# One fused two-layer kernel: the queries of head h+4 moved ahead of the scores of head h+2

## What is computed

```python
x += expert(layernorm(x), ...)      # int8-like quantised linear, SiLU gate, quantised linear
x += bitlinear_ffn(layernorm(x))    # 704 hidden units, ternary weights
x += cross_attention(layernorm(x), ctx, Wq, Wk, Wv, Wo)   # 16 heads of 128, 8 key/value heads
x += shared_ffn(layernorm(x)) + top2_routed_ffn(layernorm(x))  # 1024 hidden units, 128 routed
```

## Time and profile before

| | |
|---|---|
| median of three runs | 385.16 us |
| the profiled execution | 384.46 us |
| its span, from its first to its last instruction | 382.7 us |
| granted TensorE clock | 0.999 of full speed |
| TensorE (PE) busy | 373.5 us, 98% |
| TensorE weight loads (PEld) busy | 352.6 us, 92% |
| VectorE (DVE) busy | 299.0 us, 78% |
| ScalarE (ACT) busy | 233.8 us, 61% |
| GpSimd (POOL) busy | 163.1 us, 43% |

### The profile page before, as it was taken

How to read it: one execution, slowest core, us unless ns; L and a number is a source line. 1 busy time by engine, 2 the same in 40 slices (tenths; PEclk the granted TensorE clock), 3 DMA queues, 4 the chain that set the end, 5 groups by cost and what they waited for, 6 DMA issues and landing times.

```text
span 382.7 us, 8393 instructions
## 1 busy us (share of the span) xinstructions
PE 373.5 (98%) x2966; PEld 352.6 (92%) x2966; DVE 299.0 (78%) x983; ACT 233.8 (61%) x617; POOL 163.1 (43%) x260
## 2 busy tenths in 40 slices
PE   8899999999999999999999999999999999999996
PEld 7788799999899989999999999999999989999896
DVE  4798889899867889887867999787767876766644
ACT  1798787877644466767454567766554666764232
POOL 2113876947533345345353445246343243332232
PEclk9999999999999999999999999999999999999999
DMA  7999200000000300000000200000000000000000
GB/s 241 340 376 399 79 33 2 2 2 0 3 2 0 87 0 3 2 1 3 0 29 2 60 1 2 0 3 1 3 29 2 0 3 0 3 0 2 15 17 27
DMA packets 15193, 16.93 MB, mean 44 GB/s; under 512 B 1584, under 2 KB 14128, under 8 KB 15152
## 3 DMA queue, kind: packets, MB, share of 16 engines
q1 hardware_dynamic: 15152, 16.40, 12.8%
HBM read 15.34 MB, written 1.05 MB: 43 GB/s over the span
## 4 chain that ended last, share of the span: by engine, by line
PE 83%; DVE 9%; ACT 3%; POOL 2%; issue 1%; DVEq 0%; POOLq 0%
PE bank_qa L412 12%; PE bank_u L649 8%; PE bank_o L668 8%; PE bank_pt L633 7%; PE bank_s L613 7%; PE bank_s L412 5%; PE bank_o L672 4%; PE bank_u L653 4%; PE bank_s L621 4%; PE bank_s L531 3%; PE bank_pt L412 2%; PE bank_u L757 2%; PE bank_pt L531 2%; PE bank_x L421 2%; PE bank_pt L561 2%; PE bank_x L757 1%
## 5 line engine op out<-in xcount | busy, mean ns | idle before, releaser
L1339 POOL TENSOR_SCALAR prob<-prob,row_inv,valid_b 128x256 f32<-128x256 f32 x128 | 71.0, 566 | 82.7 <-DVE row_inv L1710 82.7
L1034 ACT ACTIVATE prob<-prob,row_min 128x256 f32<-128x256 f32 x128 | 64.1, 503 | 41.7 <-DVE row_min L1702 41.4
L1715 DVE TENSOR_TENSOR pt_lo<-bank_pt,pt_hi 128x512 fp32r<-128x512 f32 x64 | 43.8, 685 | 14.3 <-ACT pt_hi L987 14.3
L1702 DVE CUSTOM_DVE_ANT_0 prob<-bank_s,masked 128x256 f32<-128x256 f32 x128 | 48.5, 416 | 0.9 <-ACT masked L1016 0.6
L1350 POOL TENSOR_TENSOR act_lo<-act_raw,act_hi 128x256 fp32r<-128x256 f32 x32 | 24.2, 756 | 44.0 <-ACT act_hi L1102 43.9
L633 PE MATMUL bank_pt<-ident,prob 128*128 128x128 f32 x256 | 39.3, 275 | 0.6 <-DVE pt_lo L1715 0.6
L987 ACT ACTIVATE pt_hi<-bank_pt 128x512 fp32r<-128x512 f32 x64 | 37.6, 587 | 3.9 <-PE bank_pt L633 3.7
L613 PE MATMUL bank_s<-cxT_hi,qa_hi 128*128 128x256 f32 x128 | 37.7, 317 | 0.0
L412 PE MATMUL bank_qa<-xt_hi,a_hi 128*128 128x256 f32 x126 | 35.1, 279 | 0.0
L412 PE MATMUL bank_qa<-xt_lo,a_hi 128*128 128x256 f32 x126 | 35.1, 279 | 0.0
L412 PE MATMUL bank_qa<-xt_hi,a_lo 128*128 128x256 f32 x126 | 35.1, 279 | 0.0
(11 more groups left out here) (338 smaller groups left out, 1187.9 us busy)
## 6 DMA issues: line engine op xcount, KB each, us to landing
wq_raw<-in_wqT SPq DMA_DIRECT2D x4, 512.0 KB, 7.6
wo_raw<-in_wo SPq DMA_DIRECT2D x4, 512.0 KB, 7.7
w_raw<-in_w12T SPq DMA_DIRECT2D x2, 704.0 KB, 7.4
gate_raw<-in_gateT SPq DMA_DIRECT2D x2, 576.0 KB, 7.3
up_raw<-in_upT SPq DMA_DIRECT2D x2, 576.0 KB, 9.9
down_raw<-in_downT SPq DMA_DIRECT2D x2, 576.0 KB, 11.8
x<-in_x SPq DMA_DIRECT2D x4, 256.0 KB, 5.0
guT<-in_guT SPq DMA_DIRECT2D x4, 256.0 KB, 3.3
```

What stands on the lines that cost most here:

```text
L1034: act.activation(row, row, ACT.Exp, scale=-1.0, bias=row_min[:, h % 2, t:t + 1], accum_out=row_sum[:, h % 2, t:t + 1]).then_inc(S["s_exp"], 1)
L1339: pool.tensor_scalar(row, row, row_inv[:, h % 2, t:t + 1], valid_b[:, 0:1], ALU.mult, ALU.mult).then_inc(S["s_norm"], 1)
L1702: dve.tensor_tensor_reduce(out=prob[:, h % 2, t, :], in0=src[:, t * T:(t + 1) * T], in1=masked[:, :], scale=1.0, scalar=3.0e38, op0=ALU.ad ...
L1715: dve.tensor_tensor(pt_lo[:, :, cols], bank["pt"][:, :].rearrange("p (s t) -> p s t", s=2), f32(pt_hi[:, :, cols]), ALU.subtract).then_inc ...
```

## The change

In each turn of TensorE's attention loop the queries of head h+4 stand directly behind the transposes of head h, and the scores of head h+2 behind them. No instruction is added or removed, and no engine but TensorE has another order. The wait for `qa_l` in front of an even head's queries now stands ahead of the scores. The scores' own waits move with them.

```diff
@@ -677,10 +677,10 @@
 
                 for h in range(H):
                     turn_probs(b, h)
+                    if h + 4 < H:
+                        queries(b, h + 4)
                     if h + 2 < H:
                         scores(b, h + 2)
-                    if h + 4 < H:
-                        queries(b, h + 4)
                     if beside is not None:
                         beside(h, 0)
                     if h >= 2:
```

## The result

The changed kernel took 385.98 us, the median of 11 runs (385.66 to 386.71), beside 385.00 us for the kernel before in the same session. The ratio is 1.0026, with a 95% interval of 1.0018 to 1.0034: 1.0 us slower, where 0.7 was forecast. The profiled execution has a span of 383.9 us at a granted clock of 1.0, against 382.7 before.

The account below looks back on a forecast made before the run. TensorE, busy 98% of the span, was taken to bound the kernel. Terms 0.6 (batch 3) + 0.05 + 0.05 (batches 1 and 2) + 0 (batch 0) = 0.7 us, giving 385.16 + 0.7 = 385.9 us, range 384.9 to 387.0.

Parts of the forecast that it names:

- Batch 3, 0.6 us forecast: Turns 0 and 2: queries wait for `qa_lo` (0.59 and 0.34 us), minima 0.43 us late; 0.6 us stay to the end.
- The hole before turn 3: Batch 3: TensorE's idle time before the transposes of turn 3 takes back 0.2 us of its 0.79 us lateness.
- Batch 1, 0.05 us forecast: Turn 2's queries wait 0.16 us for `qa_lo`; turn 5's wait for `pt_lo` absorbs it, about 0.05 us remains.
- rival C: Late minima become the bound in the VectorE and ScalarE loop, delays are not returned: 1.6 us, 386.8 us; chance 0.21.
- Batch 2, 0.05 us: Repeats batch 1: 0.16 us pause in turn 2, absorbed in turn 5 until about 0.05 us remains.
- Batch 0, nothing: No queries in batch 0 wait longer for `qa_lo`, so it adds 0 us.
- Turn 10: Batch 0, the nearest other turn to a stall: `qa_lo` ends at 87.92, TensorE comes at 88.00, 0.03 us to spare.
- The scores moved back: Scores come 0.68 us later; turn 6 minima 0.16 us late in batches 0 to 2, hidden by 0.51 us idle in turn 7.
- The queries moved forward: ScalarE's 9.3 us of waits for query matmuls go in odd turns; gain put at nothing, at most about 1 us.
- Rival D: Early queries remove ScalarE's 0.34 us idle times and this reaches TensorE; three turns give 1.0 us: 384.2 us; chance 0.09.
- The restart: The matmul behind a wait holds up the next by some 0.11 us; a skill rule would make this free, about 0.15 less.
- The bound between same and slower: Differences up to 0.2%, 0.77 us, count as same; the forecast's middle lay just under, at 385.93 us.

Follow-up runs that it names:

- its two turns alone: The queries go ahead of the scores in turns 0 and 2 of batch 3 alone, against the kernel before: ratio 1.0016 (1.0007 to 1.0025), 0.6 us.
- odd-turns kernel: The queries go ahead of the scores in odd turns alone, against the kernel before: ratio 0.9998 (0.9990 to 1.0007).

## Why the prediction was right, and where it was off

*Batch 3, 0.6 us forecast: 0.66 and 0.62 in two profiles, and 0.6 by the clock for its two turns alone (0.48 in their trace).* The chain was as told: a pause that costs nearly nothing by itself, minima late by it, the mix waiting for `pt_hi` and `pt_lo`, a second pause of 0.35 us in turn 2 (0.34 was forecast), a part of it taken back. Most of the mix's wait is for `pt_hi`, before its first matmul (0.42 us), where the forecast put it at `pt_lo`. One link was mis-sized. I let the minima start 0.05 us after the last score matmul ends; they start 0.15 after (304.33 and 304.47 above, and 0.14 to 0.15 in 98 turns of the profiled kernels). This is most of why the delay was 0.55 and not 0.43. The hole before turn 3 gave 0.2 back as said. Then 0.1 more went at turns 5 and 6, and no hole gave it. In turn 4 the 256-column matmuls start 0.118 us apart in the kernel before and 0.113 in the changed one, and the turn takes 2.56 and 2.49 us. The odd-turns kernel, which has no pause there, shows the same 2.49. The forecast counted 0.112 throughout and had nothing for this. The 0.1 too little and this 0.1 cancel, and that is luck.

*Batch 1, 0.05 us forecast: 0.32 to 0.34. This is the step that failed.* The pause in turn 2 came as forecast (0.13 us at turn 3), and turn 5 was to take it back, because its transposes wait for a `pt_lo` that was taken to stay where it was. It did not stay. VectorE of the changed kernel in turn 2 of batch 1:

```profile
144.17 0.68 DVE L1715 TENSOR_TENSOR pt_lo<-bank_pt,pt_hi 128x512 fp32r<-128x512 f32 x1
145.05 0.42 DVE L1702 CUSTOM_DVE_ANT_0 prob<-bank_s,masked 128x256 f32<-128x256 f32 x1 [0.21 <-issue]
```

The minima start 0.88 us behind `pt_lo`, though the scores had ended at 144.56; 0.60 is usual, also in batch 2 with the scores ending at the same distance of 0.39. From here to the `pt_lo` of turn 4 VectorE has no idle time over 0.05 us to take the 0.28 back. It hands them on to `qa_lo` in turn 3 and to `pt_lo` in turn 4, and TensorE waits for both:

```profile
148.66 0.69 DVE L1683 TENSOR_TENSOR qa_lo<-bank_qa,qa_hi 128x512 fp32r<-128x512 f32 x1
148.97 0.60 PE L633 MATMUL bank_pt<-ident,prob 128*128 128x128 f32 x4
149.40 0.38 PE L412 MATMUL bank_qa<-xt_hi,a_hi 128*128 128x256 f32 x1
...
150.97 0.68 DVE L1715 TENSOR_TENSOR pt_lo<-bank_pt,pt_hi 128x512 fp32r<-128x512 f32 x1
151.71 0.66 PE L633 MATMUL bank_pt<-ident,prob 128*128 128x128 f32 x4
```

The first is the fifth wait, which the forecast did not have: the queries start 0.43 us behind the first transpose, where 0.36 is usual, 0.05 after `qa_lo` ends. The second is the one that was to absorb the lag: `pt_lo` ends at 151.65 instead of 151.32, and the transposes of turn 5 are 0.34 late. This is what rival C told of, a delay on VectorE that is not given back, in a place that it did not name. Batch 2, with no hole, gave its lag back as forecast. The hole itself is in all seven profiles of kernels with the change in that turn, and in each the minima start 0.49 to 0.50 us after the scores end, not 0.15; also in the kernel with the queries between the score parts, where both come 0.19 earlier. So it does follow the scores, but with a delay that no other turn in which the minima wait for scores has, and the trace calls it "issue". What makes it in this one place stays open.

*Batch 2, 0.05 us: 0.02.* The pause is there (0.18 at turn 3) and is given back by turn 6 (0.36 at turn 2, 0.38 at turn 6).

*Batch 0, nothing: not told from nothing.* The lag at its end is 0.01 in the first profile, but in the second it grows by 0.17 over the batch (0.31 to 0.48), with no wait for `qa_lo`. In the other kernels with the change there it grows by anything from -0.22 to 0.13. Turn 10, with 0.03 us to spare, held.

*The scores moved back: hidden, as forecast.* In turn 6 of batch 1 the minima start at 159.03 instead of 158.41, 0.28 us late beyond the 0.34 of lag, where 0.16 was forecast (the same 0.1 of the start after the scores). The idle time of turn 7 took it: the lag is 0.34 at turns 6 to 9.

*The queries moved forward: nothing, as forecast,* shown by the odd-turns kernel (0.9998, to within 0.1%). Rival D falls with it.

*The restart.* In the changed kernel the second query matmul behind the wait starts 0.23 us after the first (302.68 and 302.91) where 0.112 is usual, so the row was right to be kept. "TensorE: Matmul & The Clock Gate" of the Trainium skill, section "The mechanism", has weight loads pulled ahead of running matmuls. Here the load stands behind the wait too: it starts at 302.68 with its matmul, when none is running.

*The bound between same and slower.* The middle of the forecast lay just under it; the 0.3 us of batch 1 put the result, 0.98 us, just over it. The interval of the measurement, 0.7 to 1.3 us, holds the bound of 0.77.

No kernel that ran beats the one before. Odd turns alone and the queries between the score parts equal it, within 0.1%.

## What to carry to other kernels

Before moving a group of instructions forward on an engine that runs in order, look at the wait that it brings, and at what must now stand behind that wait. Here the pause of turn 0 cost TensorE 0.1 us by itself, since TensorE had stood idle before the next transposes anyway; the 0.55 us by which it delayed the work that the other engines feed on came back whole. Room has to be read at every reader in the loop, not at the last one: over 1 us before the transposes meant nothing for the copy in between. If a wait must move, split the group at the first instruction that needs it: here that gave the old time back, and no more.

## What the runs showed of the hardware that was not expected

VectorE starts 0.15 us after the modelled end of the TensorE matmul that it waits for (98 turns); TensorE starts 0.05 to 0.06 us after the end of a VectorE instruction (the transposes behind `pt_lo`). The direction matters.

Matmuls of 256 columns do not always start 0.113 us apart. At a granted clock of 1.00 there are stretches of some microseconds in which they start 0.118 apart. In places they come back: turns 6 to 8 of batch 1 ran so in all thirteen profiles, and the two profiles of the kernel before agree from turn 3 to turn 9 of batch 3. Elsewhere they change from execution to execution, and a run of them can be worth 0.5 us. The same twelve matmuls near the end, first and last of each, in the second and then in the first profile of the kernel before:

```profile
362.86 0.28 PE L412 MATMUL bank_pt<-yt_hi,gate_hi 128*128 128x256 f32 x1
...
364.15 0.28 PE L412 MATMUL bank_pt<-yt_hi,up_lo 128*128 128x256 f32 x1
```

```profile
362.78 0.28 PE L412 MATMUL bank_pt<-yt_hi,gate_hi 128*128 128x256 f32 x1
...
364.03 0.28 PE L412 MATMUL bank_pt<-yt_hi,up_lo 128*128 128x256 f32 x1
```

Eleven intervals take 1.29 us in the one and 1.25 in the other, and between 360 and 378 us such differences add up to 0.5 us. What causes it was not tried. For a change worth 1 us, the lag turn by turn tells more than the two spans.
